# Two waits and a table: the scatter of an expert layer waits per tile, and the choice's table of quarters is kept in f32

## The reference, cut to what matters

```
k = int(EXPERT_CAPACITY * t / e)                       # 512 tokens for each expert and sample
scores = jnp.einsum('ntd,ed->nte', x, gate_w)
probs = jax.nn.softmax(scores, axis=-1)
g, m = jax.lax.top_k(probs.transpose(0, 2, 1), k)
xin = x[batch_idx, m]
h = jax.nn.gelu(jnp.einsum('nekd,edf->nekf', xin, w1), approximate=False)
h = jnp.einsum('nekf,efd->nekd', h, w2)
out = jnp.zeros((n, t, d)).at[batch_idx, m].add(g[..., None] * h)
x = x + gb * out
```

## Time and profile before

| | us |
|---|---|
| median of 3 runs | 1870.5 (1869.12 to 1871.28) |
| profiled execution, its own time | 1872.29 |
| its span, first to last instruction | 1870.5 |
| PE busy in the span | 1724.7 (92%) |
| DVE busy | 1477.8 (79%) |
| POOL busy | 1371.7 (73%) |

### The profile page before, as it was taken

One profiled execution on the slowest core, in us unless ns is written; L12 is line 12 of the kernel. 1 busy time (PEld: TensorE's weight loads), 2 busy tenths in 40 slices (PEclk: granted clock), 3 DMA queues, 4 the chain that ended last, 5 costly groups with the idle time before them and its releaser, 6 DMA issues.

```text
span 1870.5 us, 34289 instructions
## 1 busy us (share of the span) xinstructions
PE 1724.7 (92%) x12348; PEld 1486.4 (79%) x12348; DVE 1477.8 (79%) x3114; ACT 1379.2 (74%) x2705; POOL 1371.7 (73%) x644
## 2 busy tenths in 40 slices
PE   6688999999999999999999999998876999999997
PEld 5567788887878888797888879787665888899996
DVE  3557888888888888888888888888898678766663
ACT  3468878888888888888888888887742756666663
POOL 0008899898989989899998989999998333444442
PEclk9899999999999999999999999999897999999998
DMA  4013222222132322323232132223222444555551
GB/s 194 1 29 73 61 67 69 65 62 86 50 86 65 73 64 58 89 52 84 64 74 71 50 91 60 73 57 85 72 54 82 133 109 103 133 136 135 136 136 23
DMA packets 120888, 149.88 MB, mean 80 GB/s; under 512 B 8208, under 2 KB 111120, under 8 KB 120336
## 3 DMA queue, kind: packets, MB, share of 16 engines
q1 hardware_dynamic: 108432, 130.91, 25.4%
q0 software_dynamic: 12288, 16.79, 5.2%
HBM read 121.98 MB, written 17.30 MB: 74 GB/s over the span
## 4 chain that ended last, share of the span: by engine, by line
PE 76%; POOL 7%; DVE 6%; issue 6%; ACT 3%; DMA 0%; POOLq 0%; DVEq 0%; ACTq 0%
PE po L1819 9%; PE pY L1136 9%; PE pD L1119 9%; PE ph L1819 9%; PE pA L718 6%; POOL room L1177 3%; PE pA L620 3%; PE pB L915 3%; DVE room L1168 3%; PE pB L925 3%; POOL room L1187 3%; PE pB L1215 3%; PE pB L946 2%; PE pA L646 2%; PE pA L611 2%
## 5 line engine op out<-in xcount | busy, mean ns | idle before, releaser
L1187 POOL TENSOR_TENSOR room<-room 128x1024 f32<-128x1024 f32 x256 | 606.9, 2371 | 180.6 <-DVE room L1102 143.2
L1168 DVE TENSOR_TENSOR_SCAN room<-pD,last,room 128x256 f32<-128x256 f32 x1024 | 691.7, 732 | 50.4 <-PE pD L1119 38.8
L1177 POOL TENSOR_TENSOR room<-room 128x1024 f32<-128x1024 f32 x256 | 606.5, 2369 | 64.3 <-PE pY L1136 63.4
L1149 ACT ACTIVATE room<-room,fixed,kkT 128x512 f32<-128x512 f32 x512 | 406.3, 806 | 54.3 <-PE pD L1119 52.4
L1119 PE MATMUL pD<-fixed,room 128*128 128x128 f32 x2048 | 318.6, 279 | 47.2 <-DVE room L1168 45.1
L1136 PE MATMUL pY<-fixed,room 128*128 128x128 f32 x2048 | 319.2, 280 | 15.9 <-POOL room L1177 15.9
L1119 PEld LDWEIGHTS pD<-fixed,room 128*128 128x128 f32 x2048 | 244.1, 144 | 75.0 <-issue 41.4
L1136 PEld LDWEIGHTS pY<-fixed,room 128*128 128x128 f32 x2048 | 249.2, 145 | 65.8 <-POOL room L1177 30.0
L330 POOL DMA_INDIRECT xg<-xn_rows,W x64 | 69.4, 1084 | 199.2 <-DVE W L324 184.1
L1778 ACT ACTIVATE h<-ph 128x512 f32<-128x512 f32 x128 | 76.7, 599 | 136.6 <-PE ph L1819 94.7
L1819 PE MATMUL po<-w_up,h_up 128*128 128x256 f32 x512 | 148.9, 291 | 3.2 <-DVE h_rest L1686 2.6
(11 more groups left out here) (310 smaller groups left out, 3591.0 us busy)
## 6 DMA issues: line engine op xcount, KB each, us to landing
room<-kq_rows SPq DMA_DIRECT2D x256, 256.0 KB, 5.3
w_in<-w_d SPq DMA_DIRECT2D x32, 1024.0 KB
room<-ndS SPq DMA_DIRECT2D x16, 512.0 KB, 3.3
xt<-x_in SPq DMA_DIRECT2D x16, 256.0 KB, 3.0
y_out<-xo SPq DMA_DIRECT2D x16, 256.0 KB, 2.1
xn_rows<-xnC SPq DMA_DIRECT2D x16, 256.0 KB, 2.1
W<-weights SPq DMA_DIRECT2D x1, 1808.0 KB, 9.3
W<-weights SPq DMA_DIRECT2D x1, 1697.5 KB, 16.8
```

The lines of the kernel that those rows point to most:

```text
L1149: act.activation(decT[:, m % 2, t, :], turn2(ndT, it, NT * DI, t * DI, DI), ACT.Identity, bias=ones_s[:, 0:1], scale=turn2(kkT, it, NT * D ...
L1168: dve.tensor_tensor_scan(run, pD[h][:, k2 * TB:(k2 + 1) * TB], run, last[:, bass.ds(later(it) * (DS * DT) + m * DT + k, 1)], ALU.mult, ALU ...
L1177: pool.tensor_tensor(sq[:, m % 2], st[:, m % 4], kqb[:, m % SLOTS, 1, :].unsqueeze(1).broadcast_to([P, DT, TB]), ALU.mult).then_inc(sem("r ...
L1187: pool.tensor_tensor(st[:, m % 4], turn2(u, it, DT * TB).rearrange("p (k t) -> p k t", k=DT), kqb[:, m % SLOTS, 0, :].unsqueeze(1).broadca ...
```

## The change

```diff
@@ -141,7 +141,7 @@
-             ("lo", LT, F32), ("quarter", SL * LT // 2, BF16),
+             ("lo", LT, F32), ("quarter", SL * LT, F32),
@@ -1868,10 +1868,10 @@
             def scatter(k):
-                pool.wait_ge(sem("scaled"), (k + 1) * SL)
                 if k % E == 0:
                     pool.wait_ge(sem("x_out"), ((k // E + 1) * BPB + 1) * 16)
                 for s in range(SL):
+                    pool.wait_ge(sem("scaled"), k * SL + s + 1)
                     pool.indirect_dma_start(
                         out_rows, bass.IndirectOffsetOnAxis(ap=select.ids[:, k * SL + s:k * SL + s + 1], axis=0),
                         ys[:, k % 2, s, :], None, compute_op=ALU.add).then_inc(sem(f"added{k % 2}"), 16)
```

## The result

| | before | after |
|---|---|---|
| median | 1870.76 us (6 runs, 1869.12 to 1872.77) | 1864.39 us (6 runs, 1862.30 to 1866.27) |
| span of the profiled execution | 1870.5 us | 1861.7 us |
| last scaling's start to the end of the span | 13.90 us | 8.34 us |

The ratio is 0.9968, with a 95% interval from 0.9958 to 0.9978: 6.4 us less, where 5.6 were forecast.

What follows compares the result with a forecast made beforehand. At the end only POOL's four scatter DMAs of list 15, issued one after the other, stood in the chain. 1870.5 - 5.6 (tail) + 0 (f32 table, place(0)) = 1864.9 us, 0.30% less; range 1861.8 to 1867.3.

Steps and rivals of the forecast that it cites:

- Where a scatter's wait matters: Scatter DMAs: per-tile waits cost and gain 0 in lists 0 to 14; only list 15, with nothing behind it, gains.
- The tail term, 5.58 us: List 15: the fourth scatter DMA's issue starts at 1857.36 instead of 1862.94 us, 5.58 us earlier (three times 1.86).
- the 7.56 us behind it: From the last scatter issue's start to the span's end: 1.7 to first data, 1.5 burst, 4.3 silence, all kept.
- the closing silence follows the last transfer: End of program: the last 4.3 us without data were taken to move with the last transfer; otherwise the tail gains nothing.
- L295 and L302 in f32 cost nothing: Table of quarters on DVE: f32 costs 0.01 us in each of 16, 0.2 us in all, taken as 0.
- f32 doesn't free place(0): place(0)'s 4.58 us L302 on DVE: f32 pairs with two SBUF inputs wait for POOL as well; gain 0.
- until POOL's last product: place(0): L302 in f32 was expected to wait, as before, until POOL's last product ended.
- The rival's price of 4.1 us: place(0): f32 frees L302 from its wait for POOL, 4.1 us more gain, sum 1860.8 us; chance 0.10.
- what follows comes 4.1 us sooner: Rival's step behind place(0): with L302 and L306 done early, everything after moves 4.1 us, unless POOL's work holds it.

Runs made afterwards that it cites:

- e3: The kernel before with per-tile waits in lists 0 to 14 only, single wait in list 15, bf16 table: 1869.51 us, ratio 0.9999.
- e7: The changed kernel without the scatter DMA of list 15's last tile: the span ends 4.9 us behind the end of the last scaling; no median given.
- e1: The kernel before with the per-tile waits alone, table of quarters still bf16: 1864.06 us, ratio 0.9970.
- e2: The kernel before with the table of quarters in f32 alone, one wait for four tiles as before: 1870.92 us, ratio 1.0005.
- e4: The changed kernel with eight added DVE instructions (bf16, f32 and mixed products, f32 copies) during POOL's products: products took 0.84 to 2.31 us instead of 0.42.
- e6: The changed kernel with list 0's part of place(0)'s two tables copied to a free PSUM bank and read there: 1862.47 us, ratio 0.9959.
- e10: The same kernel as e6, measured once more in another group: 1861.98 us, ratio 0.9958.
- e8: e6 with SP's load of list 1's weights held back until list 0's rows have arrived: 1860.89 us, ratio 0.9951.
- e9: The changed kernel with SP's load of list 1's weights held back until list 0's rows have arrived: 1864.12 us, ratio 0.9969.
- e5: The changed kernel once more, unaltered, measured and profiled again: 1864.24 us, ratio 0.9967 to the kernel before.

## Why the prediction was right

- **Where a scatter's wait matters.** Right: list 15 only. e3 shows the first 15 lists to be worth 0 within 0.1% (1.9 us).
- **The tail term, 5.58 us.** Right in the profile, 5.56: the fourth issue came 0.28 us behind its scaling, and the 7.56 us behind it stayed (7.58). e7 settles what the prediction had to assume, that the closing silence follows the last transfer. e1 gives the size in time, 0.9970. That the medians differ by 6.4 us and not 5.6 is within the noise.
- **L295 and L302 in f32 cost nothing.** Right: 693 ns where it was 692, median 486 where it was 485, and e2 at 1.0005. Why the all-16-bit L302 ran at the pace of f32 was read off the sum only; no run takes its broadcasts away.
- **f32 doesn't free place(0).** Right in its outcome and its cause (e2, e4). The detail "until POOL's last product" was too narrow: in some executions DVE gets in ahead of POOL's last product, and POOL waits in turn.
- **The rival's price of 4.1 us** for a freed place(0) was too high as it stood. e6 and e10 freed it by another way, and about 2 us came through. The step that failed is "what follows comes 4.1 us sooner": the issue of the four gather DMAs moved with it, but not their landing, since the weight load that the same earliness set off took their DMA engines. In e8, with that load held back, the way from place(0)'s start to the last scaling's is 417.5 us, 4.1 less than the 421.6 of after, e7 and e9.
- **8.8 us between the profiles** would have looked like a second effect. It is how executions differ: place(0) began between 1430.0 (e1) and 1434.0 us (e8) in the profiles, in no order of the edits (1434.8 in e4, which has instructions added ahead of it).

## What to carry to other kernels

A wait for a whole batch costs only where nothing else delays the consumer: count the consumer's instances that really waited (here 2 of 64), and of these price only the one with nothing behind it to hide under, here the last of the program. There, each request that can leave with its own tile takes its issue time off the end, three times 1.86 us here. And before pricing an engine that gets through earlier, look which transfers it sets off: of the 4.1 us gained at place(0), 2.6 were lost to 1 MB of weights that no one needed yet. Where two engines share a way into SBUF, one input moved to PSUM takes the wait out.

## What the runs showed of the hardware

- DVE and POOL exclude each other by whole instructions where DVE reads two tensors from SBUF and POOL's product reads SBUF too, for bf16, f32 and mixed pairs alike (e4: 0.84 to 2.31 us for 0.42). It goes both ways: a POOL product of 2.4 us took 4.05 behind DVE's L306 (e1). With one input in PSUM, L302 took 0.47 us under the same products (e6). The Trainium skill, SBUF — State Buffer (Who interferes with whom), states this rule for two SBUF inputs, and the trace agrees. The two f32 copies of e4, with one input, ended 0.15 us behind POOL's products and seem to have waited too.
- The same kernel falls into either order, DVE behind two of POOL's products (4.6 us) or behind one (2.3 us), from one execution to the next. In eight profiles of eight the first came with a granted clock of 1.00 in the matmuls that POOL's last product waits for, and the second with 0.50.
- Rows of four gather DMAs (0.5 MB) landed 1.8 to 1.9 us after their last issue, and 4.4 to 4.6 us after it where SP had issued a load of 1 MB 0.8 us ahead of the end of that issue (e1, e2, e3, e5, e6, e10). Issued 0.4 us behind it (before, after, e4, e7), the load cost the rows nothing.
- The end of an execution lay 6.0 us behind the end of the last indirect DMA's issue, 4.2 to 4.3 of these with next to no data (a DMA share of 0.01 or less), in the kernel before, the changed one and e7.
